# Two gated layers on one core: maxima, joins, gate and router steps placed anew between two attention groups

## What is computed

```
xn = layernorm(x)
s  = attention(xn)            # 16 heads of 8, causal, softmax over keys, then @ WO
g  = moe(xn)                  # 8 experts of 512, top 2 by xn @ gate, silu(x@w1)*(x@w3) @ w2
x  = x + s * silu(g)
xn = layernorm(x)
s  = recurrent(xn)            # phases by W_omega, cos/sin, running sums, layernorm, gelu MLP, + xn
g  = moe2(xn)                 # top-2 router in 8 groups of 256 tokens, 64 slots an expert, gelu, 8 experts of 688
x  = x + s * silu(g)
```

## Time and profile before

| | us |
|---|---|
| median of 3 runs | 616.33 (616.06 to 617.59) |
| the profiled execution | 612.8 |
| its span | 611.0 |
| TensorE busy in the span | 570.4 (93%) |
| DVE busy | 476.4 (78%) |
| ACT busy | 330.7 (54%) |
| GpSimd busy | 192.9 (32%) |

### The profile page before, as it was taken

How to read it: one execution, slowest core, us unless ns; L and a number is a source line. 1 busy time by engine, 2 the same in 40 slices (tenths; PEclk the granted TensorE clock), 3 DMA queues, 4 the chain that set the end, 5 groups by cost and what they waited for, 6 DMA issues and landing times.

```text
span 611.0 us, 11965 instructions
## 1 busy us (share of the span) xinstructions
PE 570.4 (93%) x3901; PEld 352.9 (58%) x3902; DVE 476.4 (78%) x1309; ACT 330.7 (54%) x602; POOL 192.9 (32%) x221
## 2 busy tenths in 40 slices
PE   2888999999999999899999998988999999999996
PEld 1444544444454544899999963544446665666554
DVE  6799889999989898455555578757899899976465
ACT  2852667676777776555555558863223642362224
POOL 1450000000254452133333310100008685688500
PEclk9897999999999999999999999999899999999999
DMA  8955727070813271211111035124011322421232
GB/s 188 226 167 206 250 71 218 2 218 2 226 37 102 61 219 23 53 50 48 48 48 48 26 89 138 71 68 125 0 47 40 97 54 39 135 76 37 87 90 69
DMA packets 55611, 57.99 MB, mean 95 GB/s; under 512 B 8650, under 2 KB 39402, under 8 KB 55514
## 3 DMA queue, kind: packets, MB, share of 16 engines
q1 hardware_dynamic: 51242, 50.56, 29.8%
q0 software_dynamic: 4320, 6.81, 3.5%
HBM read 41.96 MB, written 18.85 MB: 100 GB/s over the span
## 4 chain that ended last, share of the span: by engine, by line
PE 74%; DVE 18%; ACT 3%; issue 2%; POOL 1%; DMA 1%; SPq 1%; ACTq 0%; DVEq 0%; POOLq 0%
PE banks L1720 11%; PE banks L1863 9%; PE banks L1788 8%; PE banks L1810 7%; PE banks L1996 7%; PE banks L1732 6%; PE banks L1985 5%; PE banks L1982 5%; PE banks L2047 4%; DVE banks L1268 4%; DVE mpart L1271 3%; PE banks L1791 2%; PE banks L1872 1%; POOL rows_a L613 1%; PE banks L1681 1%
## 5 line engine op out<-in xcount | busy, mean ns | idle before, releaser
L828 ACT ACTIVATE arena<-banks 128x512 f32<-128x512 f32 (+1 forms) x304 | 153.8, 582 | 71.9 <-PE banks L1791 39.6
L1268 DVE CUSTOM_DVE_ANT_0 banks<-banks,arena 128x512 f32<-128x512 f32 (+3 forms) x256 | 120.0, 513 | 9.1 <-PE banks L1810 8.1
L1810 PE MATMUL banks<-arena 96*128 96x512 bf16 (+3 forms) x384 | 114.1, 340 | 4.1 <-DVE mpart L1268 2.3
L1788 PE MATMUL banks<-arena 128*128 128x512 bf16 (+3 forms) x384 | 115.5, 332 | 2.6 <-ACT arena L828 1.8
L1271 DVE TENSOR_REDUCE mpart<-banks 128x1 f32<-128x512 f32 x128 | 85.9, 685 | 9.1 <-PE banks L1810 8.0
L1720 PE MATMUL banks<-arena 128*128 128x128 f32 x624 | 76.3, 275 | 1.0 <-ACT arena L762 1.0
L1720 PEld LDWEIGHTS banks<-arena 128*128 128x128 f32 x624 | 72.8, 192 | 1.5 <-ACT arena L762 1.5
L1863 PE MATMUL banks<-arena 128*9 128x512 f32 (+3 forms) x768 | 70.8, 487 | 0.0
L870 ACT ACTIVATE arena<-banks 125x512 f32<-125x512 f32 (+2 forms) x48 | 28.5, 595 | 71.3 <-PE banks L1982 46.3
L1788 PEld LDWEIGHTS banks<-arena 128*128 128x128 bf16 x384 | 37.9, 99 | 46.2 <-issue 23.4
L639 POOL DMA_INDIRECT results<-arena x39 | 37.8, 969 | 77.4 <-DVE arena L1156 77.4
(11 more groups left out here) (297 smaller groups left out, 857.3 us busy)
## 6 DMA issues: line engine op xcount, KB each, us to landing
k_parts<-arena SPq DMA_DIRECT2D x6, 768.0 KB, 8.1
arena<-in_L_ffn_experts_w_dram SPq DMA_DIRECT2D x2, 2048.0 KB, 10.8
arena<-results SPq DMA_DIRECT2D x8, 512.0 KB, 6.5
arena<-k_parts SPq DMA_DIRECT2D x7, 576.0 KB
arena<-q_parts SPq DMA_DIRECT2D x28, 144.0 KB
arena<-in_L_ffn_w_kernel_dram SPq DMA_DIRECT2D x8, 344.0 KB, 3.8
slots<-in_pad_rows_dram SPq DMA_DIRECT2D x1, 2535.0 KB, 12.2
arena<-slots SPq DMA_DIRECT2D x39, 65.0 KB, 1.8
```

The lines of the kernel that those rows point to most:

```text
L828: act.activation(Pr[:, r % 4, heads[0]:heads[-1] + 1, 0:n], banks[:, E_BANK[e], 0:len(heads) * n].rearrange("p (j c) -> p j c", j=len(head ...
L1268: ins = dve.tensor_tensor_reduce(unmasked, unmasked, tail_mask[:, 512 - n:512], 1.0, -BIG, ALU.add, ALU.max, part[:, at:at + 1])
L1788: ins = pe.matmul(banks[:, E_BANK[e], at * n:at * n + n], QK[:, slot, j, 1, P * kt:P * kt + P], QK[:, slot, j, 0, q:q + n], start=True, st ...
L1810: ins = pe.matmul(ps[:, at * n:at * n + n], QK[0:TALL, slot, j, 0, P * i:P * i + P], QK[0:TALL, slot, j, 1, 512 * half:512 * half + n], st ...
```

## The change

Three things are moved.

1. Behind `experts0` the remaining maxima of group 7 (first pass) are no longer put after each exponential as fast as the count before allowed (they ended at exponential 36 of group 6), but in equal shares over 36 exponentials (with the empty places that the stream counts at its end); the last one stands behind exponential 3 of group 7. `negmax` for the second half goes from exponential 36 of group 6 to 3 of group 7, its `maxrow` from 4 to 9.
2. The joins (`combine`) of the first layer are done by GpSimd and no longer by DVE. The gate of the first half moves from exponential 32 to 38 of group 6; the gate of the second half leaves the list and stands on ACT behind its last exponential and last evacuation. `finish` goes from 36 and 37 of group 6 to 10 of group 7, `norm` from 1 and 3 to 11 and 12 of group 7, `x_turn` from 16 and 17 to 21 and 23, `route_exp` and `logits1` from 21 and 22 to 26 and 27, `places1` from 31 to 35. The attention output moves by one exponential.
3. On TensorE, behind the last group, the bias products stand in front of `places1` and not behind it.

The number of matmuls, maxima and exponentials stays the same. The Silu of the second half is a table load of its own now: in the list one Silu stands between two loads as two did before, and one more load stands behind the last exponential.

```diff
--- before.py
+++ after.py
@@ -99,10 +99,11 @@
 SPREAD_BANK = (1, 3, 0, 2)
 SCATTER_AT, SCATTER_EVERY = 3 * EXP_UNITS + 20, 3
 EXPERTS_AT = (6, 3)
-MIDDLE = {2: [("attn_turn", 0)], 4: [("attn_turn", 1)], 7: [("attn_out", 0)], 9: [("attn_out", 1)],
-          16: [("combine", 0)], 19: [("combine", 1)], 21: [("gate", 0), ("gate", 1)], 25: [("finish", 0)], 26: [("finish", 1)],
-          28: [("norm", 0)], 30: [("norm", 1)], 43: [("x_turn", 0)], 44: [("x_turn", 1)], 48: [("route_exp",), ("scale",)],
-          49: [("logits1",), ("route_max",), ("route_choice",)], 58: [("places1",), ("route_places",)]}
+MIDDLE = {2: [("attn_turn", 0)], 4: [("attn_turn", 1)], 8: [("attn_out", 0)], 10: [("attn_out", 1)],
+          20: [("combine", 0)], 24: [("combine", 1)], 27: [("gate", 0)], 37: [("finish", 0), ("finish", 1)],
+          38: [("norm", 0)], 39: [("norm", 1)], 48: [("x_turn", 0)], 50: [("x_turn", 1)], 53: [("route_exp",), ("scale",)],
+          54: [("logits1",), ("route_max",), ("route_choice",)], 62: [("places1",), ("route_places",)]}
+MAXIMA_OVER = 36
 MAX_TILES = ((3, 0, 2, 1), (7, 4, 6, 5))
 OPENING, LEAD, ROW_DELAY, POOL_DELAY = 22, 40, 3, 6
 SECOND = {2: [("project", 4)], 3: [("project", 5)], 4: [("values", 2)], 7: [("project", 6)], 8: [("project", 7)], 10: [("values", 3)]}
@@ -147,6 +148,7 @@
 
 
     stream = maxima_stream()
+    maxima_in_all = sum(step[0] in ("p1", "pad") for step in stream)
     place = [0, 0]
 
     def maxima(upto):
@@ -173,7 +175,10 @@
             for i, step in enumerate(exps):
                 plan.append(step)
                 n += 1
-                plan += maxima(OPENING + (LEAD + half0 - OPENING) * n // half0 if n < half0 else n + LEAD)
+                if since is not None:
+                    plan += maxima(begun + (maxima_in_all - begun) * min(since + 1, MAXIMA_OVER) // MAXIMA_OVER)
+                else:
+                    plan += maxima(OPENING + (LEAD + half0 - OPENING) * n // half0 if n < half0 else n + LEAD)
                 plan += routing_step(k, pair)
                 if since is not None:
                     since += 1
@@ -191,7 +196,7 @@
                 plan.append(("turn", k, 0))
             if (k, r) == EXPERTS_AT:
                 plan.append(("experts0",))
-                since = 0
+                since, begun = 0, place[1]
         plans[k] = plan
     return plans
 
@@ -672,6 +677,10 @@
                         negated(*step[1:])
                     elif step[0] == "experts0":
                         experts0()
+                    elif step[0] == "combine":
+                        tiles = slice(8 * step[1], 8 * step[1] + 8)
+                        pool.wait_ge(ld_y[step[1]], 32)
+                        pool.tensor_tensor(ya[:, tiles, :], ya[:, tiles, :], yb[:, tiles, :], ALU.add).then_inc(Z["f_done"], 1)
 
             pool.wait_ge(Z["pads1_in"], 32)
             pool.wait_ge(Z["pv_done"], NG * NS)
@@ -850,6 +859,7 @@
 
 
 
+            gate_half(0, 1)
             for c in range(2, 4):
                 act.wait_ge(Z["aT_ps"], c - 1)
                 act.copy(attnT[:, 512 * c:512 * c + 512], psM[:, c % 2, :]).then_inc(Z["aT_sb"], 1)
@@ -1324,8 +1334,6 @@
                         unit += 1
                     elif step[0] == "experts0":
                         experts0()
-                    elif step[0] == "combine":
-                        combine(ld_y[step[1]], 32, step[1])
                     elif step[0] == "attn_turn":
                         c = step[1]
                         dve.tensor_copy(attnT0[:, 512 * c:512 * c + 512], unit_ready()).then_inc(Z["aT0_sb"], 1)
@@ -1949,11 +1957,11 @@
             pe.wait_ge(Z["ld_L1"], 16 * 6)
             phases(1)
             phases(2)
-            places1(1, psM[:, 1, :])
             for o in range(2):
                 for c in range(4):
                     ins = pe.matmul(psO[:, o:o + 1], W1g[:, c, P * o:P * o + P], vecs[:, 6 + c:7 + c], start=(c == 0), stop=(c == 3))
             ins.then_inc(Z["cb_ps"], 1)
+            places1(1, psM[:, 1, :])
             pe.wait_ge(Z["lg_sb"], 5)
             phases(0)
             pe.wait_ge(Z["disp_sb"], 4)
```

## The result

The changed kernel takes 623.02 us (median of 4 runs, 621.89 to 627.03) where the kernel before took 616.96 beside it (4 runs, 616.06 to 617.63): a ratio of 1.0086, 95% interval [1.0046, 1.0127]. Two more measurements of the same kernel gave 1.0068 [1.0046, 1.0090] and 1.0058 [1.0036, 1.0080]. So the change costs 0.6 to 0.9%. The forecast was no change, 616.7 us, with a range that ended at 619.0: it was wrong, on the slow side.

What follows compares the result with a forecast made beforehand. TensorE was taken as the bound (busy 46.72 of 50.00 us), with 3.28 us of waits to win back. +1.3 at the last turn and -0.9 from the bias products sum to +0.4: 616.7 us for 616.33, range 613.8 to 619.0.

Steps and rivals of the forecast that it cites:

- Part 1: Up to exponential 38 of group 6: spread maxima, GpSimd joins, gates; a 1.4 us stall replaces a 1.79 us wait.
- The gate's stall: TensorE at group 7's fifth exponential product waits 1.4 us, as ACT spends 3.6 us on two loads and a Silu.
- Part 2: Group 7, exponential 12: the late row of maxima holds TensorE 1.7 us until 388.7, leaving 0.5 us won.
- The stand: TensorE's wait at exponential 12 of group 7 for the DMA of the row of maxima: 1.7 us (1.1 to 2.3).
- Part 3: Router and one-hots, group 7: places1 comes at 403.0, DVE's one-hots end late, last turn +1.3 us.
- The banks' wait: Late in group 7, exponential products 32 and 33 wait 0.6 us for their banks, behind ACT's router exponential.
- Part 4: Second-half gate behind ACT's last evacuation: load and Silu take 2.3 us, hidden with 0.9 us to spare.
- the drain that part 4 cites: Drain added to each ACT table load, a switch about 2.66 us; the gate would end at 411.3, 0.5 us late.
- Part 5: Behind the last group: bias products in front of the counts fill TensorE's 1.52 us wait; -0.9 us (-1.2 to -0.5).
- Slower: Rival: group 6's turn reaches DVE 2 us late, delaying the chain through logits1, places1, one-hots; 618.7 us; chance 0.20.
- Faster: Rival: the 1.4 us gate and 1.7 us maxima-row stalls don't appear, last turn -1.7 us; 613.7 us; chance 0.26.
- The joins don't leave the path: Rival: GpSimd's join lands after the first-half gate asks at 377.6; two us late give 618.7; chance 0.02.

Runs made afterwards that it cites:

- The run that moved the two steps: Changed kernel with logits1 (with the router's exponential and scale) and places1 two steps earlier: 614.16 us beside 614.60, ratio 1.0002.
- the kernel made late: Kernel before with three more one-hots of the same values on DVE in front of its four: 1.0059; with bias products in front of the counts too, 1.0050.
- the joins': Kernel before with only the two joins moved from DVE to GpSimd: ratio 1.0009.
- all three cures: Changed kernel with bias products behind the counts, three of four one-hots behind the last turn, seven unused products before TensorE's wait for the last group: 1.0037.
- late one-hots: Changed kernel with three of the first half's four one-hots moved on DVE behind the last turn: 1.0029; with four unused TensorE products added, 0.9999.

## Why the prediction was wrong

**Part 1** held. The gate's stall was 1.50 us for 1.4 forecast, the joins took GpSimd 2.36 us for 2.3, the early one ended at 371.55 and the later at 375.15, and the gate on ACT began at 378.75, which less the offset of 0.75 is 378.0 for 377.6:

```profile
378.75 1.28 ACT L817 ACT_TABLE_LOAD   x1
380.04 1.06 ACT L817 ACTIVATE arena<-arena 128x1024 f32<-128x1024 f32 x1
381.12 1.28 ACT L837 ACT_TABLE_LOAD   x1
...
400.75 0.26 ACT L808 ACTIVATE rt<-rt 128x64 f32<-128x64 f32 x1 [2.08 <-DVE rt L1223]
...
412.56 0.58 ACT L865 COPY arena<-banks 128x512 f32<-128x512 f32 x1 [0.77 <-PE banks L1930]
```

**Part 2** held, with one error that didn't matter. The DMA of the row of maxima took 2.20 us on the chain, 2.4 estimated:

```profile
387.35 2.20 DMA arena<-arena
```

The 12th exponential product began at 389.60 (388.85 less the offset, forecast 388.7). The stand was 1.02 us and not 1.7: TensorE came 0.8 later to it than I had walked, and the DMA ended both.

**Part 3 is the term that was mis-sized**: +1.3 us forecast, +2.32 measured. The step that failed is "TensorE took 399.93 - 389.26 = 10.7 us for exponentials 12 to 31 and what lies between them; the same steps now end at 388.7 + 10.7". The work is the same and its pace is not. In the chain of waits of the kernel before (start, us, what) this stretch runs over DVE's rows of the norm until 391.20 and over TensorE behind that

```profile
391.90 0.77 PE banks L1863 x16
392.67 1.19 PE banks L1788 x5
393.85 1.69 PE banks L1913 x16
```

and in that of the changed kernel over ACT, for exponential after exponential until 394.06, and over TensorE only behind it:

```profile
391.47 0.45 ACT arena L837
...
393.37 0.69 ACT arena L837
...
394.50 0.44 PE banks L1624 x4
```

Before, the two turns of x and logits1 stood among the first eleven of these exponentials, 0.6, 0.66 and 1.7 us of TensorE in which ACT, at about 0.5 us an exponential, could catch up. Now ten exponentials follow each other with one set of value products among them, so ACT sets the pace. That is read from the two chains; no run moved the turns of x alone. logits1 ended at 399.95, less 0.75 is 399.2, for the forecast 398.5: 0.15 us of the 0.7 is the later start of exponential 12, and 0.55 the slower pace. The banks' wait was 0.59 for 0.6; with 0.3 us more behind it places1 came at 404.74, less 0.75 is 404.0, for the forecast 403.0. From there the 6.5 us to the end of the one-hots were right (404.74 to 411.32 in the trace), and DVE was directly behind them with the last turn, as forecast. So the mechanism was named and its size was short by 1.0 us. The run that moved the two steps shows that their places make the turn late: it takes 1.95 of the 2.32 us back. It leaves the ACT-paced stretch in front of logits1 as it was (exponential 12 begins 31.62 us behind the zero, 31.61 in the changed kernel), so it doesn't test the pace itself. The forecast had written them down as fixed places of the plan and had never asked what two places earlier would bring.

**Part 4** held. The gate ended at 411.79 and the copy behind it waited 0.77 us longer for TensorE (the last ACT row above). That the delay of part 3 is its cover was right as well: in the kernel with the two steps earlier the copies follow the gate at once, at 412.39, and TensorE waits 0.90 us before its output products for 0.68. The load of 1.28 us is followed by its function 0.01 us later here too, so the drain that part 4 cites is not seen.

**Part 5** (-0.9 us) is not borne out. Where the clock held, the last turn to the experts took 31.06 (bias products alone), 30.87 and 30.88 us, which is 1.0 to 1.2 less than the 32.03 that it reckoned from. But the 32.03 had 1.8 us of lost clock in it, and the unchanged kernel's second profile, with as much lost, has 31.13. In the three comparisons of means, the bias products in front leave the rest at +0.1 alone, 0.4 lower in the kernel made late (1.9 for 2.3), and no lower in the changed kernel (1.9 and 2.5 for 2.0). In the changed kernel's profiled execution the stretch took 35.50.

**What the forecast left out is the clock.** It prices the longer stand before the attention turns (1.74 for 0.68 us) at its own length, and nothing of it speaks of what TensorE does behind it, though the kernel before already shows its clock at 0.91 in 420 to 440. Of the 3.7 and 3.2 us that the repeats lost on the mean, 1.8 and 0.7 go with the clock; the rest of 1.9 and 2.5 is about the last turn's +2.3 and leaves nothing for part 5's -0.9. The forecast's range would have held +2.3 alone (616.33 + 2.3 = 618.6); with 0.7 to 1.8 for the clock it is 619.3 to 620.4, outside. The first measurement is not wholly accounted for. It lost 6.8 us on the mean of four executions at a clock of 0.972; if the kernel before beside it had the 0.981 or 0.982 of the other chips, 3.1 to 3.5 us are the clock's part and the rest of 3.3 to 3.7 is more than the +2.3.

Of the rivals, *Slower* had the right chain (DVE from logits1 over places1 to the one-hots) and the wrong place of the lateness: not the turn of group 6 (385.9 with the offset for 385.3), behind which TensorE shows no wait at the first turn of x, but ACT's pace behind exponential 12 and the places given to logits1 and places1. *Faster* failed as its own objections said: 2.5 of the 3.1 us of stalls appeared. *The joins don't leave the path* didn't occur.

**The experts' end** (+3.32 in the profiled pair) can't be laid to the change: the changed kernel has been seen without it (5.74 us) and the unchanged one with it (7.86). DVE's copy of the last expert result waits 10.30 us with no releaser of its own core in the row, and 5.74 us for TensorE in the kernel before. Over the sixteen later profiles it goes by the chip: on two chips all eight, the unchanged kernel's and the joins' among them, waited 7.48 to 10.44 us, on the other two chips all eight waited 5.73 or 5.74. The chips of the first pair are not on record. The cause stays open.

## What to carry to other kernels

When steps are moved in a hand-written order, ask for each stretch between two of them which engine will set its pace without what stood there: a long product on one engine may be the other's time to catch up, and a duration read with it in place is no price for the stretch without it. Where a chain (router, counts, one-hots) ends in front of work that all else waits for, try its steps two places earlier before judging the rest of the plan. And a longer stand of TensorE ahead of a dense stretch may cost more than its length (here +3.5 and +3.0 us for a turn 1.98 later); for a difference below 1% compare many executions' times together with their mean clocks, since one profile may have it either way.

## What the chip showed that I had not expected

- One us of full clock lost goes with about 0.57 us of time: 0.354 us for 0.001 of mean clock, which in a span of 615 us is 0.62 us lost. This is a correlation over executions, not a cost measured by itself.
- In the changed kernel, also with its bias products moved back, the same 1.74 us wait was followed by half clock in three profiled executions (3.4, 3.4 and 1.8 us of full clock lost in 400 to 420) and by full clock in a fourth. What decides it stays open. With unused products in the gap the mean clock stood higher against the kernel before beside it (+0.0007 for -0.0020 to -0.0051 in the changed kernel, and +0.0050 for +0.0014 with the steps earlier), but not in the kernel before (0.0000) and not with all three cures (-0.0013).
- A second half-clock stretch, begun between 426 and 432 us, came in eleven of eighteen profiles, with the long wait and without it; nothing here says what brings it.
- Filling a wait with useless products went with a time 0.25 to 0.35% lower where the wait was 1.74 us, 0.3% lower with late one-hots (wait 0.68), and 0.2% or nothing lower in the two others with 0.68. Only the 0.2% was measured on one chip, and its intervals overlap.
- The wait of DVE before the last expert result's copy, 1.7 to 4.7 us longer on some chips than on others, with the same kernel.
